# The edge stage of a graph attention layer rewritten: direct gather indices, four slots, messages in place, half-rows with their weights, and the carried row as one more edge

## Chip, core and metric

The kernel runs on one core of a Trainium2 chip. The metric is the device time of one execution in microseconds (us), the median of several runs. The engines named below are TensorE (PE), VectorE (DVE), ScalarE (ACT), GpSimd (POOL) and SyncE (SP); SP and POOL issue the DMAs of this kernel.

## The reference

6250 nodes with 512 features, 100000 edges sorted by their destination `dst`, with random sources `src`. Everything is f32. After the graph layer stands a small per-node network, which the change touches only where it reads the sums.

```python
h = leaky_relu(layernorm(x) @ W.T + b, 0.2).reshape(N, 8, 64)
e_src = sum(h * w_att_src, -1);  e_dst = sum(h * w_att_dst, -1)
e = leaky_relu(e_src[src] + e_dst[dst], 0.2)
m = segment_max(e, dst);  ex = exp(e - m[dst]);  s = segment_sum(ex, dst)
a = ex / s[dst] * dist
x = x + segment_sum(h[src] * a[:, :, None], dst).reshape(N, 512)
# then x = x + ffn(layernorm(x)): decode, three small layers, one-hot codes added
```

## The kernel before, in words

Three stages follow one another, with a short preparation between the first two.

**Nodes** (`project`, 49 tiles of 128 nodes): layer norm, the 512x512 product, leaky relu, and the two scores of each head. A row of 520 f32 (512 values and 8 source scores, 2080 bytes) goes to the table `h` in HBM. `prepare` then computes, for each group of edges, the first destination (`bases`), every edge's destination relative to it (`rel`), and a table of shifts for each node (`shifts`).

**Edges** (`attend_windows`): 112 groups of 7 tiles of 128 edges. All destinations of a group lie in one window of 128 nodes that begins at the group's base. For a group g the engines do this:

- ACT copies 7 columns of source indices into `src_idx` (`set_src`). POOL waits for that copy, then issues 7 indirect DMAs (L768), each of which fetches 128 rows of `h` into a slot of `gathered`. There are three slots. From the fourth group on POOL also waits until the messages of the group that had the slot are made.
- DVE compares node numbers with `rel` and gives the 0/1 matrix `member16` (L778, bf16, 128x896). ACT widens it to f32 (`member`), PE transposes it (L873), ACT copies the transpose (`turn_member`, `memberT`), and PE multiplies it with the window of shifts (`at_edges`, L864), which looks up the destination's numbers for every edge.
- DVE sums the three bf16 parts of that result (`at_dst`, L786), adds the source scores, makes the leaky relu and the difference; ACT takes the exponential `ex` and splits off its bf16 parts together with DVE (L819, L824); DVE makes the coefficients and seven messages into a buffer of its own (`w_msg`, L810).
- PE adds up (`add_up`): per tile an f32 product of `member` and the 512 message columns (L886, recorded as two passes a tile), and then seven small bf16 products for the sums of the weights (L893).
- ACT takes the sum out of PSUM into `summed` (`evacuate`), DVE reduces the three parts of the weights into it (L831), and then adds the first row of the next window as it stood in HBM (`carried`, L841): two groups' windows overlap in one node, and SP loads that one row (L752) after the store of the group before has landed (L751). SP then stores 128 rows into `agg` (L741). So there is a chain from group to group: `carried` -> store -> landing -> load of one row -> landing -> `carried`.

Each engine has a fixed order for one round u: ACT `set_src(u+1)`, `exps(u-1)`, widen(u), exponent part (u-1), `turn_member(u)`, `evacuate(u-3)`; PE `at_edges(u-1)`, first half of `add_up(u-2)`, transposes(u), second half of `add_up(u-2)`; DVE `carried(u-4)`, scores(u-1), member(u), messages(u-1), weights(u-3); SP window load(u), row load(u-4), store(u-4). The first nine groups and the last four are written out; between them a loop of three groups a turn runs.

**Finish** (13 chunks of up to 4 tiles): divides by the sum of the weights, adds to x, and runs the small network, with f32 products on PE (L1197, L1208).

Of the kernel before, what the change touches and what calls it, by code (L numbers as in the profile page):

```python
# [22 lines left out]
P = 128  # L23
# [9 lines left out]
ROW = D + HEADS  # L33
GROUP = 7
GROUPS = -(-E // (P * GROUP))
# [20 lines left out]
CHUNKS = NODE_TILES // CHUNK  # L56

# [49 lines left out]
def project(nc, top, banks, t, keep):  # L107

    with ExitStack() as ctx:
# [49 lines left out]
        with nc.Block() as block:  # L159
# [40 lines left out]
            def _(pool):  # L200
# [3 lines left out]
                for n, s in turns(pool, NODE_TILES):  # L204
# [3 lines left out]
                    nc.gpsimd.tensor_tensor(prod_dst[:, s, :], hrow[:, s, 0:D], w_dst[:, :],  # L208
# [3 lines left out]
            def _(dve):  # L212
# [17 lines left out]
                def scores(n, s):  # L230
# [6 lines left out]
                    nc.vector.tensor_tensor(hrow[:, s, 0:D], leak[:, s, :], ps_h[s][:, :], ALU.max).then_inc(s_row, 1)  # L237
# [3 lines left out]
                    nc.vector.tensor_tensor(prod_src[:, :], hrow[:, s, 0:D], w_src[:, :], ALU.mult  # L241
                                            ).then_inc(s_psrc, 1)
                    dve.wait_ge(s_psrc, n + 1)
                    nc.vector.tensor_reduce(hrow[:, s, D:ROW], prod_src[:, :].rearrange("p (h d) -> p h d", h=HEADS),
                                            AX, ALU.add).then_inc(s_esrc, 1)
# [54 lines left out]
            def _(act):  # L300
# [12 lines left out]
                def keep_src(n, s):  # L313
                    act.wait_ge(s_esrc, n + 1)
                    nc.scalar.activation(keep["esrc"][:, bass.ds(n * HEADS, HEADS)], hrow[:, s, D:ROW], ACT.Copy
                                         ).then_inc(s_kept, 1)
# [18 lines left out]
def attend_any(nc, top, banks, t, keep, branch_semaphores):  # L335
# [3 lines left out]
    with ExitStack() as ctx:  # L339
# [50 lines left out]
        with nc.Block() as block:  # L390
# [31 lines left out]
            def _(dve):  # L422
                dve.wait_ge(s_load, 16)

                def heads(ap):
                    return ap.rearrange("p (h d) -> p h d", h=HEADS)

                for n in edge_turns(dve):
# [5 lines left out]
                    if reused(n, 1):  # L434
# [22 lines left out]
                    step("score", nc.vector.tensor_tensor(score[:, :], grow[:, D:ROW], mrow[:, HEADS:2 * HEADS],  # L457
                                                          ALU.add))
# [7 lines left out]
                    for b in range(2):  # L466
# [4 lines left out]
                        if b == 0:  # L471
# [17 lines left out]
                    nc.vector.tensor_tensor(heads(msg[:, :]), heads(grow[:, 0:D]),  # L489
                                            coef[:, :].unsqueeze(2).to_broadcast([P, HEADS, HD]), ALU.mult  # L490
                                            ).then_inc(done["msg"], 1)
                    dve.wait_ge(s_a, 16 * (n + 1))
                    nc.vector.tensor_tensor(heads(arow[:, 0:D]), heads(arow[:, 0:D]),
                                            exps[:, 0:HEADS].unsqueeze(2).to_broadcast([P, HEADS, HD]),
                                            ALU.mult).then_inc(s_scaled, 1)
# [149 lines left out]


def attend_windows(nc, top, banks, t, keep, branch_semaphores):

    with ExitStack() as ctx:
        def sb(name, shape, dt=F32):
# [850 lines left out]
```

## Time and profile before

| | us |
|---|---|
| median of 3 runs | 2029.5 |
| lowest and highest | 2019.91 and 2036.35 |
| the profiled execution: its own time | 2030.48 |
| its span, first to last instruction | 2028.7 |
| node stage and preparation, in the span | 0 to 354 |
| edge stage | 354 to 1718 |
| finish | 1718 to 2028.7 |

The durations that follow come from the one profiled execution. Its own time is 1.8 us above its span and 1.0 us above the median. The edge stage takes 1364 of the 2028.7 us, 12.18 us for each of 112 groups. The mean granted clock of TensorE over the span was 0.852 of full speed.

### The profile page before, as it was taken

Reading aid. Unit: us, or ns where it says so; the run is one execution under the profiler, and the core shown is the slowest. Engines: PE = TensorE matmul, PEld = TensorE weight load, DVE = VectorE, ACT = ScalarE, POOL = GpSimd, SP = SyncE. Lnnn points to the kernel's source line nnn. Section 1 sums busy time; section 2 is a strip of 40 time slices with the busy share of each in tenths; the row PEclk is TensorE's granted clock in tenths of the full one; section 3 lists DMA queues with packets and bytes.
Section 4 is the critical chain, followed back from the end, with each engine's and each line's share of the span. In section 5 each row is a group of like instructions: output and inputs, shape, how many; then the busy total and the mean of one; then the engine's idle time right before and its main releaser. Section 6 shows DMA issues by size and latency. Waiting matters only on the chain. (4 is left out here: it accounts for less than half of the span.)

```text
span 2028.7 us, 24635 instructions
## 1 busy us (share of the span) xinstructions
PE 1406.5 (69%) x5502; PEld 662.8 (33%) x5502; DVE 1337.0 (66%) x3092; ACT 496.3 (24%) x1141; POOL 986.9 (49%) x932
## 2 busy tenths in 40 slices
PE   5778783477666676566767676766657665299997
PEld 2333331233232233232323232323223332155555
DVE  5777776467566576665766576666657655868784
ACT  1222220222222222222322222222222221123332
POOL 1222221666656566575556755666666651213231
PEclk9999987688888898888888888888889878578888
DMA  5333333666665566575566765666666653424331
GB/s 216 131 124 126 125 125 64 166 195 191 176 175 172 169 191 191 168 200 168 160 172 194 199 171 159 191 178 174 172 188 182 188 165 91 176 89 167 145 135 67
DMA packets 151399, 326.44 MB, mean 161 GB/s; under 512 B 47312, under 2 KB 47568, under 8 KB 151246
## 3 DMA queue, kind: packets, MB, share of 16 engines
q0 software_dynamic: 62720, 208.78, 37.1%
q1 hardware_dynamic: 88654, 117.38, 17.2%
q8 instruction: 9, 0.15, 0.0%
q14 instruction: 16, 0.13, 0.0%
HBM read 255.82 MB, written 70.27 MB: 161 GB/s over the span
## 5 line engine op out<-in xcount | busy, mean ns | idle before, releaser
L768 POOL DMA_INDIRECT gathered<-table_h,w_src_idx x784 | 827.5, 1055 | 517.2 <-issue 244.3
L886 PE MATMUL bank<-w_msg,member 128*128 128x512 f32 x1568 | 810.3, 662 | 0.0
L810 DVE TENSOR_TENSOR w_msg<-gathered,w_coef 128x512 f32<-128x512 f32 x784 | 489.8, 694 | 3.9
L886 PEld LDWEIGHTS bank<-w_msg,member 128*128 128x128 f32 x1568 | 313.8, 213 | 316.3 <-issue 282.2
L873 PE MATMUL bank<-ident,member 128*128 128x128 bf16 x784 | 72.0, 240 | 313.8 <-DVE member L778 221.2
L786 DVE TENSOR_REDUCE at_dst<-bank 128x112 f32<-128x336 f32 x112 | 56.3, 503 | 326.8 <-remote 259.5
L277 PE MATMUL bank<-wt,xnT 128*128 128x512 f32 x392 | 203.0, 666 | 0.0
L208 POOL TENSOR_TENSOR prod_dst<-hrow,w_dst 128x512 f32<-128x512 f32 x49 | 75.6, 1543 | 250.4 <-DVE hrow L237 250.4
L920 ACT ACTIVATE w_ex<-w_diff 128x56 f32<-128x56 f32 x112 | 27.9, 249 | 673.2 <-issue 348.0
L873 PEld LDWEIGHTS bank<-ident,member 128*128 128x128 bf16 x784 | 53.5, 108 | 402.6 <-DVE member L778 221.4
L1197 PE MATMUL bank<-h,w 128*128 128x512 f32 (+1 forms) x338 | 180.3, 682 | 0.0
L841 DVE TENSOR_TENSOR summed<-summed,w_carry 1x520 f32<-1x520 f32 x111 | 76.4, 688 | 155.7 <-ACT summed L908 126.4
L1114 POOL TENSOR_TENSOR res<-x_in,y 128x2048 f32<-128x2048 f32 (+1 forms) x13 | 61.9, 4765 | 234.9 <-DMA out<-res 162.8
L908 ACT ACTIVATE memberT<-bank 128x896 bf16<-128x896 bf16 x112 | 102.1, 911 | 266.0 <-remote 239.3
L778 DVE TENSOR_TENSOR member<-node_no,k_rel 128x896 bf16<-128x896 f32 x112 | 122.1, 1090 | 9.6 <-DMA node_no<-in_node_no 9.6
L908 ACT ACTIVATE member<-member 128x896 f32<-128x896 bf16 x112 | 106.5, 951 | 64.0 <-issue 35.0
L864 PE MATMUL bank<-window,memberT 128*128 128x48 bf16 x784 | 40.3, 190 | 117.4 <-ACT memberT L908 94.8
L277 PEld LDWEIGHTS bank<-wt,xnT 128*128 128x128 f32 x392 | 78.0, 209 | 95.7 <-issue 95.7
L1197 PEld LDWEIGHTS bank<-h,w 128*128 128x128 f32 x338 | 68.8, 223 | 64.3 <-issue 62.3
L286 PE MATMUL bank<-ident,xn 128*128 128x128 f32 x196 | 32.3, 289 | 78.7 <-DVE xn L227 78.7
L1143 ACT ACTIVATE h<-bank,b 128x512 f32<-128x512 f32 (+1 forms) x65 | 41.7, 661 | 162.7 <-PE bank L1208 90.6
L1208 PEld LDWEIGHTS bank<-w,h 128*128 128x128 f32 x490 | 72.0, 225 | 21.7 <-issue 20.9
(133 smaller groups left out, 1185.8 us busy)
## 6 DMA issues: line engine op xcount, KB each, us to landing
table_agg<-summed SPq DMA_DIRECT2D x112, 260.0 KB
table_agg<-zeros SPq DMA_DIRECT2D x50, 260.0 KB, 2.2
table_h<-hrow SPq DMA_DIRECT2D x49, 260.0 KB, 2.1
xt<-in_x SPq DMA_DIRECT2D x49, 256.0 KB, 2.7
gathered<-table_h,w_src_idx POOLq DMA_INDIRECT x784
agg_in<-table_agg SPq DMA_DIRECT2D x12, 1040.0 KB, 7.7
x_in<-in_x SPq DMA_DIRECT2D x12, 1024.0 KB, 5.4
out<-res SPq DMA_DIRECT2D x12, 1024.0 KB, 4.4
```

The lines of the kernel that those rows point to most:

```text
L208: nc.gpsimd.tensor_tensor(prod_dst[:, s, :], hrow[:, s, 0:D], w_dst[:, :], ALU.mult).then_inc(s_pdst, 1)
L277: mm = nc.tensor.matmul(ps_h[s][:, :], xnT[:, s, c * P:(c + 1) * P], wt[:, c, :], start=False, stop=(c == DC - 1))
L768: pool.indirect_dma_start(out=gathered[:, s, j, :], out_offset=None, in_=t["h"][:, :], in_offset=bass.IndirectOffsetOnAxis(ap=src_idx[:, s ...
L778: nc.vector.tensor_tensor(member16[:, s, :, :], node_no[:, :].unsqueeze(1).to_broadcast([P, GROUP, P]), keep["rel"][:, bass.ds(g * GROUP, ...
L810: nc.vector.tensor_tensor(msg[:, s, j, :].rearrange("p (h d) -> p h d", h=HEADS), gathered[:, s, j, 0:D].rearrange("p (h d) -> p h d", h=H ...
L841: nc.vector.tensor_tensor(summed[0:1, s, :], summed[0:1, s, :], carry[:, :], ALU.add).then_inc(d["carried"], 1)
L873: last = nc.tensor.transpose(member_t[:, j * P:(j + 1) * P], member16[:, s, j, :], ident16[:, :])
L886: nc.tensor.matmul(sums[s][:, :], member[:, s, j, :], msg[:, s, j, :], start=first, stop=final)
L908: return nc.scalar.activation(out, in_, ACT.Copy)
L1114: nc.gpsimd.tensor_tensor(res[:, s, 0:k, :], x[:, s, 0:k, :], y[:, s, 0:k, :], ALU.add).then_inc(d["res"], 1)
L1197: last = nc.tensor.matmul(bank[:, 0:w], w2[:, weights, :], h1[:, units, 0:w], start=(i == 0), stop=(i == len(pairs) - 1))
L1208: last = nc.tensor.matmul(y3[:, 8 * j:8 * j + 8], h2[:, g, j * P:(j + 1) * P], w3[:, g, :], start=(g == 0), stop=(g == 4))
```

## The change

- The two halves of a row carry their own weights: a row is 2 x (256 values + 4 scores), still 520 f32. `project` and `finish` read and write it through split views.
- POOL gathers straight from the index table; the copy `src_idx` and the wait for it are gone. It waits for the sums of the group that had the slot. There are four slots.
- The exponentials go into the four score columns of each half of the gathered row, and the messages overwrite the gathered values in place. PE then adds up values and weights in one product for each half: two f32 products of 260 columns a tile in place of one of 512 and one small bf16 one. The bf16 parts of `ex`, L819, L824, L831 and L893 are gone.
- The carried row becomes an edge: slot 32 of tile 0 in each group stays free of edges (895 edges a group, still 112 groups), its `rel` is set to 0, and SP loads the row of `agg` into `gathered[32, slot, 0]` after the message of tile 0 is made. PE adds tile 0 last, when that row has landed. L841 is gone.
- The lookup (member, transposes, `at_edges`) runs one group ahead of the scores, with two PSUM banks for its result. The operands `coef` and `node_no` move to PSUM.
- All rounds are written out, without a loop. The window load runs two groups ahead.

The diff, cut to its core:

```diff
             def _(pool):
-                for g, s in rounds(pool, 0):
-                    wait_alone(pool, s_idx, g + 1, s_pool_on)
+                for g in range(GROUPS):
+                    s = g % S
                     if old(g):
-                        wait_alone(pool, d["msg"], GROUP * (g - 2), s_pool_on)
+                        wait_alone(pool, d["sums"], g - S + 1, s_pool_on)
                     for j in range(GROUP):
                         pool.indirect_dma_start(
                             out=gathered[:, s, j, :], out_offset=None, in_=t["h"][:, :],
-                            in_offset=bass.IndirectOffsetOnAxis(ap=src_idx[:, s, j:j + 1], axis=0)
-                        ).then_inc(s_g[s], 48)
+                            in_offset=bass.IndirectOffsetOnAxis(ap=keep["src"][:, g, j:j + 1], axis=0)
+                        ).then_inc(s_g[s], 16)
...
+                def carry_in(g, s):
+                    to = gathered[CARRY_ROW:CARRY_ROW + 1, s, 0, :]
...
+                    base = base_of(g)
+                    before = (s - 1) % S
+                    sp.wait_ge(s_put[before], filled(g - 1, 16))
+                    sp.wait_ge(d["msg"], g * GROUP + 1)
+                    sp.dma_start(to, t["agg"][bass.ds(base, 1), :]).then_inc(s_carry, 16)
+
+                for u, slot in rounds(2, 1):
+                    stage(u, slot, -2, load_window)
+                    stage(u, slot, 1, store)
+                    stage(u, slot, 0, carry_in)
...
                     for j in range(GROUP):
+                        values = row_values(gathered[:, s, j, :])
                         nc.vector.tensor_tensor(
-                            msg[:, s, j, :].rearrange("p (h d) -> p h d", h=HEADS),
-                            gathered[:, s, j, 0:D].rearrange("p (h d) -> p h d", h=HEADS),
-                            coef[:, j, :].unsqueeze(2).to_broadcast([P, HEADS, HD]), ALU.mult
-                        ).then_inc(d["msg"], 1)
+                            values, values, by_half(coef[:, j * HEADS:(j + 1) * HEADS]).unsqueeze(3)
+                            .to_broadcast([P, 2, HEADS // 2, HD]), ALU.mult).then_inc(d["msg"], 1)
...
+                for u, slot in rounds(1, 0):
+                    stage(u, slot, 0, scores)
+                    stage(u, slot, -1, make_member)
+                    stage(u, slot, 0, messages)
...
+                def add_tile(g, s, j, start, stop):
+                    for a in range(2):
+                        last = nc.tensor.matmul(sums_of(s)[:, a, :], member[:, s, j, :],
+                                                gathered[:, s, j, a * HALF:(a + 1) * HALF], start=start, stop=stop)
+                    return last
+
+                def add_first(g, s):
+                    pe.wait_ge(d["member"], g + 1)
+                    if old(g, 2):
+                        pe.wait_ge(d["evac"], g - 1)
+                    for j in range(1, 5):
                         pe.wait_ge(d["msg"], g * GROUP + j + 1)
+                        add_tile(g, s, j, j == 1, False)
+
+                def add_rest(g, s):
+                    for j in range(5, GROUP):
+                        pe.wait_ge(d["msg"], g * GROUP + j + 1)
+                        add_tile(g, s, j, False, False)
+                    pe.wait_ge(s_carry, 16 * (g + 1))
+                    add_tile(g, s, 0, False, True).then_inc(d["sums"], 1)
 
                 pe.wait_ge(s_i16, 1)
+                for u, slot in rounds(1, 0):
+                    stage(u, slot, -1, transpose)
+                    stage(u, slot, 0, add_first)
+                    stage(u, slot, -1, at_edges)
+                    stage(u, slot, 0, add_rest)
...
+                for u, slot in rounds(1, 1):
+                    stage(u, slot, 0, exps)
+                    stage(u, slot, 1, evacuate)
+                    stage(u, slot, -1, widen_member)
+                    stage(u, slot, -1, turn_member)
```

## Rows read from the trace of the kernel before

**Rows 1.** The page, part 1: busy time, share of the span and instructions of each engine.

```profile
PE 1406.5 (69%) x5502; PEld 662.8 (33%) x5502; DVE 1337.0 (66%) x3092; ACT 496.3 (24%) x1141; POOL 986.9 (49%) x932
```

**Rows 2.** Busy time in the edge stage: PE, PEld, DVE, ACT, POOL, clock, DMA share, GB/s.

```profile
354.00:1718.00 1364.00, 902.70 (x3920) 412.37 (x3920) 862.32 (x1903) 343.62 (x786) 827.45 (x784) 0.85 0.62 176
```

**Rows 3.** Groups of instructions: busy us, mean ns of one | idle before, its enders.

```profile
L768 POOL DMA_INDIRECT gathered<-table_h,w_src_idx x784 | 827.5, 1055 | 517.2 <-issue 244.3 <-DVE w_msg L810 149.0 <-ACT w_src_idx L908 123.9
L886 PE MATMUL bank<-w_msg,member 128*128 128x512 f32 x1568 | 810.3, 662 | 0.0
L810 DVE TENSOR_TENSOR w_msg<-gathered,w_coef 128x512 f32<-128x512 f32 x784 | 489.8, 694 | 3.9
L886 PEld LDWEIGHTS bank<-w_msg,member 128*128 128x128 f32 x1568 | 313.8, 213 | 316.3 <-issue 282.2 <-DVE w_msg L810 34.0
...
L841 DVE TENSOR_TENSOR summed<-summed,w_carry 1x520 f32<-1x520 f32 x111 | 76.4, 688 | 155.7 <-ACT summed L908 126.4 <-issue 11.6 <-DVE summed L831 10.0
...
L908 ACT ACTIVATE summed<-bank 128x512 f32<-128x512 f32 x112 | 66.2, 591 | 10.0 <-PE bank L893 10.0
...
L893 PE MATMUL bank<-w_ex,member 128*128 128x24 bf16 x784 | 37.3, 174 | 56.1 <-issue 30.3 <-DVE summed L831 25.8
...
L819 DVE TENSOR_TENSOR w_ex_rest<-w_ex 128x56 f32<-128x56 f32 x112 | 23.3, 208 | 0.6 <-ACT w_ex L908 0.6
```

**Rows 4.** Waits in the edge stage: us in total, times, longest us.

```profile
DVE at_dst L786 <- remote: 259.5, 42, 13.1
...
ACT memberT L908 <- remote: 239.3, 48, 12.1
```

**Rows 5.** The timeline of PE: start us, us, instruction, count, [idle before].

```profile
514.10 0.19 PEld L886 LDWEIGHTS bank<-w_msg,member 128*128 128x128 f32 x1 [0.24 <-issue]
...
516.58 0.34 PE L864 MATMUL bank<-window,memberT 128*128 128x48 bf16 x7
...
550.37 0.56 PE L873 MATMUL bank<-ident,member 128*128 128x128 bf16 x7 [1.08 <-issue]
```

**Rows 6.** The timeline of POOL in the same stretch.

```profile
527.09 0.95 POOL L768 DMA_INDIRECT gathered<-table_h,w_src_idx  x1 [0.30 <-issue]
537.27 1.10 POOL L768 DMA_INDIRECT gathered<-table_h,w_src_idx  x1 [9.23 <-DVE w_msg L810]
```

**Rows 7.** The timeline of DVE and of ACT: what waited for those PE instructions.

```profile
529.59 0.51 DVE L786 TENSOR_REDUCE at_dst<-bank 128x112 f32<-128x336 f32 x1 [12.37 <-remote]
...
532.14 4.30 DVE L810 TENSOR_TENSOR w_msg<-gathered,w_coef 128x512 f32<-128x512 f32 x7
...
558.91 0.92 ACT L908 ACTIVATE memberT<-bank 128x896 bf16<-128x896 bf16 x1 [7.39 <-remote]
```

**Rows 8.** The timeline at the stage's start: first and seventh gather, first scores.

```profile
356.80 1.70 POOL L768 DMA_INDIRECT gathered<-table_h,w_src_idx  x1 [16.93 <-issue]
...
365.07 0.95 POOL L768 DMA_INDIRECT gathered<-table_h,w_src_idx  x1 [0.30 <-issue]
...
368.95 0.51 DVE L786 TENSOR_REDUCE at_dst<-bank 128x112 f32<-128x336 f32 x1 [11.61 <-DMA gathered<-table_h,w_src_idx]
```

**Rows 9.** The timeline: store and row load of SP twice, then the last L841.

```profile
892.61 0.42 SPq L741 DMA_DIRECT2D table_agg<-summed  x1
...
897.32 0.06 SPq L752 DMA_DIRECT2D w_carry<-table_agg  x1
...
1713.48 0.42 SPq L741 DMA_DIRECT2D table_agg<-summed  x1
1715.76 0.28 SPq L752 DMA_DIRECT2D w_carry<-table_agg  x1
...
1717.21 0.69 DVE L841 TENSOR_TENSOR summed<-summed,w_carry 1x520 f32<-1x520 f32 x1 [2.87 <-DMA w_carry<-table_agg]
```

**Rows 10.** The timeline of PE in the finish: twenty f32 passes of 8 columns.

```profile
1909.40 2.40 PE L1208 MATMUL bank<-w,h 128*128 128x8 f32 x20
```

More of the change, by code:

```diff
@@ L32 @@
 DC = D // P
[L33 removed]
+HALF = D // 2 + HEADS // 2
+ROW = 2 * HALF
 GROUP = 7
[L35 removed]
+CARRY_ROW = 32
+GROUP_EDGES = P * GROUP - 1
+GROUPS = -(-E // GROUP_EDGES)
 EDGE_TILES = GROUPS * GROUP
@@ L691, in attend_windows @@
-        s_g = [sem(f"w_gathered{i}") for i in range(S3)]
-        s_put = [sem(f"w_stored{i}") for i in range(S3)]
-        s_carry = sem("w_carry_copied")
-        s_win = [sem(f"w_window_loaded{i}") for i in range(S3)]
-        names = ("member16 member member_t memberT edge_dst at_dst score leaky diff ex ex_hi ex_rest ex_mid ex_lo "
-                 "coef msg sums evac evac_w carried").split()
-        d = {k: sem("w_" + k) for k in names}
-        def filled(g, slot, per):
-            return (g - slot) * (per // S3) + per
@@ new lines, in attend_windows, with filled, sums_of, edge_dst @@
+        names = ("member16 member member_t memberT edge_dst at_dst score leaky diff ex coef msg sums evac").split()
+        d = {k: sem("w_" + k) for k in names}
+        def filled(g, per):
+            return per * (g // S + 1)
+        def sums_of(slot):
+            return psum[:, 2 * (slot % 2):2 * (slot % 2) + 2, 0:HALF]
+        def edge_dst(slot):
+            return psum[:, 6 + slot % 2, 0:GROUP * PARTS]
+        def rounds(lead, drain):
+            for u in range(-lead, GROUPS + drain):
+                yield u, u % S
@@ L713, in stage, with old @@
         def stage(u, slot, lag, do):
-            if isinstance(u, int) and not 0 <= u - lag < GROUPS:
+            if not 0 <= u - lag < GROUPS:
                 return
-            do(u - lag, (slot - lag) % S3)
-        def old(g):
-            return reused(g, S3)
+            do(u - lag, (slot - lag) % S)
+        def old(g, slots=S):
+            return g >= slots
         with nc.Block() as block:
@@ L754, in _ @@
-                for u, slot in rounds(sp, 4):
-                    stage(u, slot, 0, load_window)
-                    stage(u, slot, 4, load_carry)
-                    stage(u, slot, 4, store)
-                for g in range(GROUPS - S3, GROUPS):
-                    sp.wait_ge(s_put[g % S3], filled(g, g % S3, 48))
+                    base = base_of(g)
+                    if old(g, 1):
+                        before = (s - 1) % S
+                        sp.wait_ge(s_put[before], filled(g - 1, 16))
@@ L868, in transpose @@
                 def transpose(g, s):
                     pe.wait_ge(d["member16"], g + 1)
-                    if not (isinstance(g, int) and g == 0):
+                    if old(g, 1):
                         pe.wait_ge(d["memberT"], g)
@@ L898, in _, with at_edges @@
-                pe.wait_ge(s_i16, 1)
-                for u, slot in rounds(pe, 2):
-                    stage(u, slot, 1, at_edges)
-                    stage(u, slot, 2, lambda g, s: add_up(g, s, 0))
-                    stage(u, slot, 0, transpose)
-                    stage(u, slot, 2, lambda g, s: add_up(g, s, 1))
+                def at_edges(g, s):
+                    pe.wait_ge(d["memberT"], g + 1)
+                    pe.wait_ge(s_win[s], filled(g, 16))
+                    if old(g, 2):
+                        pe.wait_ge(d["at_dst"], g - 1)
+                    for j in range(GROUP):
+                        last = nc.tensor.matmul(edge_dst(s)[:, j * PARTS:(j + 1) * PARTS], memberT[:, s, j, :],
+                                                window[:, s, :], start=True, stop=True)
+                    last.then_inc(d["edge_dst"], 1)
```

291 lines of the change are left out of this document (110 added, 181 removed).

## The prediction

> **What bounds the kernel now.** I read the page first: no engine is full, PE 69% and DVE 66% of the span [rows 1]. Such means hide the stages, so I asked for the busy times of each stage. In the edge stage PE works 902.7, DVE 862.3 and POOL 827.5 of 1364 us, the DMA engines 0.62 of the time [rows 2]. Nothing is busy for two thirds of 12.18 us a group, so the pace comes from waits, and the list of waits [rows 4] is what the reader has to look at.
>
> POOL's own time is this. An indirect DMA takes 1.055 us on average and is followed by 0.29 us of idle time put down to issue: 244.3 us [rows 3] less the 16.9 us before the very first [rows 8], over 784. So seven take 7 x 1.345 = 9.4 us. When nothing else runs they come 1.25 us apart (0.95 and 0.30, the rows of 365.07 and 527.09 [rows 6, 8]), which is 8.75 us a group. The other 272.9 us are waits: 149.0 for the messages of the group that had the slot and 123.9 for ACT's copy of the indices [rows 3], 2.4 us a group. 9.4 + 2.4 = 11.9, and the rest of the 12.18 is the fill and the drain.
>
> Behind both waits stands a third thing. DVE's `at_dst` waits 259.5 us and ACT's `memberT` 239.3 us for something that the profile calls remote, which here means a semaphore change that it can't put beside the end of an instruction [rows 4]. Both wait for PE. The seven products L864 are recorded from 516.58 to 516.92, and `at_dst`, which needs them, starts at 529.59; the transposes of 550.37 to 550.93 are followed by `memberT` at 558.91 [rows 5, 7]. In the first case POOL issued gathers without a pause until 528.04, stopped because the messages (they begin 2.6 us after the scores and take 4.3 us [rows 7]) were not made, and went on at 537.27 [rows 6]. So PE's results are reported late while gathers run, up to 13 us, and the report comes soon after the run of gathers has ended. I can't tell the mechanism from this trace. It costs 498.8 us of waits in 90 pieces, 4.45 us a group, of which before only a part lies on the path.
>
> At the Trainium skill, SBUF — State Buffer, "Who interferes with whom", PE never waits on anyone and DMA never contends with a compute engine. By that rule nothing of these 498.8 us comes from the gathers, and a change of slots would leave them. The rows show late PE results in the edge stage and can't say of which port or queue they come, so I take the rule neither for nor against.
>
> **The change, part by part, in the edge stage.** I count the pace T of a group and then 112 T.
>
> POOL. The copy of the indices and its wait (123.9 us) go, and nothing takes their place: the table is in SBUF before the stage. The wait for the messages becomes a wait for the sums of g-4. After the late report of the example the old kernel needed 7.7 us until POOL went on (529.59 to 537.27, scores and messages of that group) [rows 6, 7]. In the new one the sums of the group four back are already added up when the stall begins, and only their report is late, so POOL goes on right after it. What stays of such a gap is the time from the last gather's end to the report, 1.5 us in the example, and some of what ACT and DVE then do. I allow 1 to 4 us and take 2.5. With 2.5 us for each of some 45 stalls (half the 90 pieces, as both engines wait in a stall) that is 112 us or 1.0 us a group, in place of 2.4.
>
> How long the gathers themselves take: between 8.75 us bare and 9.4 us as now. The excess of 0.11 us on the mean DMA is spent where DVE works, and DVE loses L841 (76.4 us) [rows 3]; I take the middle, 9.1 us. At the Trainium skill, SBUF — State Buffer, "Who interferes with whom", a `tensor_tensor` with one input in PSUM leaves GpSimd's port free, and descriptor generation is held up by two-port copies, not by `tensor_tensor`. By it `node_no` in PSUM changes nothing for the gathers and 9.4 would stay, 34 us more in all.
>
> DVE loses L841 (0.69 us), L819 (0.21) and L824 and L831, which are of L819's size or less: about 1.3 us a group [rows 3]. It keeps 862.3 - 141 = 721 us, 6.4 us a group [rows 2], with seven messages of 0.69 us as the largest part. In place or from PSUM they cost what they cost now, give or take 0.05 us each, since nothing of their shape changes; at worst 0.35 us a group, beneath POOL.
>
> PE loses L893 (37.3 us). A tile's two passes of 512 columns become four of 260. At full clock a 512-column pass is 0.43 us (0.19 of a load and 0.24 until the next [rows 5]; the load, 213 ns on average [rows 3], lies beside it), so 260 columns are 0.22 us and 28 of them 6.1 us, against 6.0 now. That holds if the weight load, which is now done 28 times, hides behind 260 columns. Twenty f32 passes of 8 columns take 2.40 us, 0.12 each [rows 10], and there is nothing in them but loads: a load needs 0.12 us of the array, about half of 0.22. I take it as hidden, with 28 x 0.12 = 3.4 us a group as the other end. With the transposes and lookups, 0.56 + 0.34 us [rows 5], PE has 7.0 us a group, or 10.4 at that other end.
>
> ACT loses `src_idx` and two small copies, and isn't near the path.
>
> The new chain from group to group, which now runs through PE, is the new cost. After the sums of g-1: ACT takes them out, 0.59 us [rows 3], and SP issues the store some 0.2 us later (an estimate, half the 0.42 us of an issue [rows 9]). From store to row load it is 2.3 us at the end of the stage, where no gather runs (1713.48 to 1715.76), and 4.7 in the midst of them (892.61 to 897.32) [rows 9], though this second one has a window load between the two. From the row load to its use it is 1.45 us at the end [rows 9]; in the midst of gathers I have no clean row, and bound it by 1.45 and 2.4 us (longer by as much as the store, 2.4, would be 3.85 at the very most). Then PE adds tile 0, 4 x 0.22 = 0.9 us. The sum is 5.4 us quiet and 0.59 + 0.2 + 4.7 + 2.0 + 0.9 = 8.4 us loaded. Under 9.1 it is hidden behind the gathers, but with little to spare, and PE's late reports now stand inside it: the wait of ACT's `evacuate` for the sums, which holds `widen` and `turn` of the next group behind it on ACT, and PE's own wait for the row, behind which the next group's transposes stand. That ordering is what the lookup one group ahead has to pay for: it gives DVE scores that don't wait for PE in the same round, and hides stalls of up to about one group's messages (4.3 us).
>
> The row layout in `project` and `finish` changes no size: messages split over 8 heads and plain 512-column operations take the same 0.69 us now. I cost it at nothing, with +-5 us for the split views. Code without a loop: the first nine groups were written out already and no slower, +-5 us. The waits of SP on its queue: behind the store's wait stand the window load two groups ahead and the row load, and neither is late by that.
>
> **The sum.** Outside the edge stage 2028.7 - 1364 = 664.7, and 1.8 between span and time. The stage begins 3 us before the first gather. After the last gather come 3.9 us to the scores (365.07 to 368.95 [rows 8]), 2.6 us to the first message and 4.3 us of messages [rows 7], and one chain of 5.4 us: 16 us. Time = 666.5 + 19 + 112 T. With T = 9.1 + 1.0 = 10.1: 685.5 + 1131 = 1817 us, and I say 1820. The profiled execution stands 1.0 us above the median, which is nothing here.
>
> **Rivals.**
> 1. PE's weight loads don't hide. T = 10.4 by PE alone, and with 1.0 us of what a stall leaves 11.4; halfway, 10.9: 1906 us. For it: 28 loads of 0.19 to 0.21 us in passes of 0.22. Against it: the 0.12 us of the array. At the Trainium skill, TensorE: Matmul & The Clock Gate, "Part 3: Packing small matmuls", loads overlap with running matmuls only when their row groups differ, and that is this rival; the trace's loads, recorded inside passes spaced 0.43 us [rows 5], speak against it.
> 2. Slower: the chain through PE takes the place of the waits removed. Each late report is paid in full, once a group, since sums, store, row and sums follow on each other: 8.4 + 4.45 = 12.85, 2125 us. It decides from T = 12.0, that is from 3.6 us of late reports a group in the chain. For it: longer runs of gathers, since four slots let POOL run ahead up to 28 gathers, and late reports come in long runs. Against it: not each late report is that of the sums, and a stall fills slots that are then worked off at 8.4 or less.
> 3. The change doesn't do what it says: the late reports set the pace as before (PE reports only when the gathers stop, so groups in a run come at the pace of stalls), T = 11.9 to 12.2, 2018 to 2052 us, within 1%.
> 4. Late reports vanish with the waits: T = 8.75 to 9.1, 1665 to 1705 us. It is the low end of the forecast.
>
> **Numbers.** About 1% is what a measurement of this kernel can tell from no change. Forecast with its low end (T from 8.9 to 10.7, 1680 to 1885): 0.66. Rival 1 (T up to 11.4, 1885 to 1960): 0.14. Rival 3: 0.06, within 1%. Rival 2: 0.14, slower. Faster by over 1% 0.80, within 1% 0.06, slower 0.14. The range of 8 in 10 is that of the forecast and rival 1, 1680 to 1960.
>
> **What would show it.** POOL's gathers should come to 1.25 to 1.35 us apart, with idle time beyond that of 1 us a group put down to the sums; DVE's busy time in the stage near 720 us; L841, L819, L824, L831 gone; f32 passes near 0.22 us apart at full clock, and the granted clock above 0.85 of the stage. If passes come 0.34 us apart, rival 1 is right. If SP's stores follow each other at the same 12 us as before, with PE waiting for the row load, rival 2 is. The prediction fails if late reports are caused by something that the new order makes worse, as I only know when they happen and not why.

## The result, and the profile after

The changed kernel took 1942.51 us (median of 4, 1933.15 to 1954.28), the kernel before 2024.7 us beside it. The ratio is 0.9626, with a 95% interval of 0.953 to 0.9722: faster, by some 80 us and not by the 210 forecast. The profiled execution took 1940.52 us. The page, part 1, of the changed kernel:

```profile
PE 1412.5 (73%) x6286; PEld 968.7 (50%) x6286; DVE 1211.7 (62%) x2647; ACT 439.4 (23%) x805; POOL 901.2 (46%) x932
```

The edge stage now lies from 352 to 1638 us (columns as in [rows 2]):

```profile
352.00:1638.00 1286.00, 915.06 (x4704) 721.52 (x4704) 736.67 (x1457) 286.42 (x450) 741.68 (x784) 0.87 0.66 188
```

POOL's 827.5 us of [rows 2] are 741.7, DVE's 862.3 are 736.7: both saved what they were meant to. The stage got only 78 us shorter. The groups of instructions, to be read beside [rows 3]:

```profile
L879 PE MATMUL bank<-gathered,member 128*128 128x260 f32 x3136 | 845.1, 426 | 110.0 <-DVE gathered L843 75.7 <-issue 30.1 <-ACT member L908 2.4
L800 POOL DMA_INDIRECT gathered<-table_h,k_src x784 | 741.7, 946 | 525.4 <-issue 237.6 <-PE bank L879 144.7 <-remote 143.1
```

A gather takes 946 ns where it took 1055, the bare value. The two waits of POOL that the change removed (149.0 and 123.9 us) are gone, and 144.7 + 143.1 = 287.8 us stand in their place, both for the sums of PE: the first where the profile finds the report beside the end of PE's last product, the second where it doesn't. The list of waits, beside [rows 4] (us in total, times, longest):

```profile
DVE at_dst L818 <- remote: 328.6, 53, 21.9
...
POOL gathered L800 <- PE bank L879: 144.7, 42, 5.6
POOL gathered L800 <- remote: 143.1, 55, 5.5
```

POOL waits 42 + 55 = 97 times in 112 groups, so now nearly every group has its stall. The timeline shows one cycle (start us, us, instruction, [idle before]):

```profile
1049.16 0.95 POOL L800 DMA_INDIRECT gathered<-table_h,k_src  x1 [2.35 <-remote]
...
1051.73 3.16 PE L879 MATMUL bank<-gathered,member 128*128 128x260 f32 x12
...
1056.66 0.95 POOL L800 DMA_INDIRECT gathered<-table_h,k_src  x1 [0.30 <-issue]
1059.22 0.60 ACT L908 ACTIVATE summed<-bank 128x520 f32<-128x520 f32 x1 [5.69 <-remote]
...
1060.00 0.94 POOL L800 DMA_INDIRECT gathered<-table_h,k_src  x1 [2.39 <-remote]
```

PE's last pass of the sums ends at 1054.89. ACT, which by its order waits for these sums next, goes on at 1059.22, 1.6 us after POOL's seven gathers have ended (1057.61), and POOL goes on 0.8 us later. One cycle is 8.45 + 2.39 = 10.84 us. Now and then a stall is long, as in this stretch:

```profile
1008.43 3.74 PE L879 MATMUL bank<-gathered,member 128*128 128x260 f32 x16 [0.63 <-ACT summed L908]
...
1012.02 0.34 PE L872 MATMUL bank<-window,memberT 128*128 128x48 bf16 x7
...
1020.59 0.94 POOL L800 DMA_INDIRECT gathered<-table_h,k_src  x1 [0.30 <-issue]
1024.12 0.51 DVE L818 TENSOR_REDUCE at_dst<-bank 128x112 f32<-128x336 f32 x1 [12.84 <-remote]
...
1025.02 0.94 POOL L800 DMA_INDIRECT gathered<-table_h,k_src  x1 [3.49 <-remote]
```

The lookup is done at 1012.36; `at_dst` starts 11.8 us later, 2.6 us after a run of gathers has ended that is longer than one group's.

### The profile page after: what moved, and what is told of

Same layout as the page of the kernel before. It is cut to its first block and busy times, and to the rows that moved or that the text cites. A ratio compares the mean times of both kernels' runs of the same rounds, so it can differ in the third digit from the quotient of the medians.

```text
span 1938.9 us, 22591 instructions
## 1 busy us (share of the span) xinstructions
PE 1412.5 (73%) x6286; PEld 968.7 (50%) x6286; DVE 1211.7 (62%) x2647; ACT 439.4 (23%) x805; POOL 901.2 (46%) x932
## 5 line engine op out<-in xcount | busy, mean ns | idle before, releaser
L800 POOL DMA_INDIRECT gathered<-table_h,k_src x784 | 741.7, 946 | 525.4 <-issue 237.6
L879 PE MATMUL bank<-gathered,member 128*128 128x260 f32 x3136 | 845.1, 426 | 110.0 <-DVE gathered L843 75.7
L879 PEld LDWEIGHTS bank<-gathered,member 128*128 128x128 f32 x3136 | 643.1, 212 | 241.3 <-issue 73.3
L843 DVE TENSOR_TENSOR gathered<-gathered,bank 128x512 f32<-128x512 f32 x784 | 478.7, 683 | 3.8
L912 ACT ACTIVATE gathered<-w_diff 128x56 f32<-128x56 f32 x112 | 27.9, 249 | 786.0 <-DVE w_diff L831 397.4
L317 PE MATMUL bank<-wt,xnT 128*128 128x512 f32 x392 | 199.0, 655 | 0.0
L811 DVE TENSOR_TENSOR member<-bank,k_rel 128x896 bf16<-128x896 f32 x112 | 121.3, 1083 | 0.0
L908 ACT ACTIVATE summed<-bank 128x520 f32<-128x520 f32 x112 | 67.1, 599 | 154.2 <-remote 112.4
L326 PEld LDWEIGHTS bank<-ident,xn 128*128 128x128 f32 x196 | 21.9, 143 | 115.6 <-DVE xn L266 69.1
```

Of the source, the lines that this page charges most:

```text
L317: mm = nc.tensor.matmul(ps_h[s][:, :], xnT[:, s, c * P:(c + 1) * P], wt[:, c, :], start=False, stop=(c == DC - 1))
L800: pool.indirect_dma_start(out=gathered[:, s, j, :], out_offset=None, in_=t["h"][:, :], in_offset=bass.IndirectOffsetOnAxis(ap=keep["src"][ ...
L811: nc.vector.tensor_tensor(member16[:, s, :, :], node_no.unsqueeze(1).to_broadcast([P, GROUP, P]), keep["rel"][:, g * GROUP:(g + 1) * GROUP ...
L843: nc.vector.tensor_tensor(values, values, by_half(coef[:, j * HEADS:(j + 1) * HEADS]).unsqueeze(3) .to_broadcast([P, 2, HEADS // 2, HD]), ...
L879: last = nc.tensor.matmul(sums_of(s)[:, a, :], member[:, s, j, :], gathered[:, s, j, a * HALF:(a + 1) * HALF], start=start, stop=stop)
L908: return nc.scalar.activation(out, in_, ACT.Copy)
```

## The experiments

The theory after the first result, the **lock**: while POOL issues gathers, PE's completion reports are held back, and come some 1.5 us after the run of gathers ends. Since POOL now starts a group on such a report, POOL and PE wait for each other once a group. Rivals: the chain through the carried row sets the pace; the traffic of the gathers, and not their issuing, holds the reports back. No run took POOL's wait for the sums away, which would have tried the lock itself.

The runs came in seven sets, each on one chip with the kernel before beside them. I hadn't expected what the sets did: in two of them the kernel before took 2000 and 1999 us, in five 1806 to 1812, and every kernel of a set followed. Chips 6 and 10 each gave one set of either kind, so it is not the chip alone. I call them **late sets** (as the first measurement) and **prompt sets**, by what the traces show: in each trace of a late set there are waits put down to "remote", in none of a prompt set.

| kernel | late sets: us, ratio to before (95%) | prompt sets: us, ratio to before (95%) |
|---|---|---|
| changed | 1918.5, 0.9617 (0.9531 to 0.9703) | 1650.5, 0.9128 (0.9083 to 0.9173) |
| no carried row | 1913.6, 0.9632 (0.9526 to 0.9737) | 1655.4, 0.9191 (0.9135 to 0.9247) |
| 80 B rows | 1938.0, 0.9729 (0.9637 to 0.9821) | 1667.2, 0.924; 1662.2, 0.9205 |
| operands in SBUF | 1917.4, 0.9615; 1912.5, 0.9641 | 1729.7, 0.9534 (0.9488 to 0.958) |
| direct indices only | 2037.6, 1.0209 (1.0101 to 1.0316) | 1807.8, 1.0014 (0.9985 to 1.0043) |
| rows issued by SP | none | 1691.9, 0.9382; 1692.0, 0.9368; 1688.1, 0.9359; 1687.6, 0.9311 |
| plain copies on POOL | none | 1797.2, 0.992 (0.9878 to 0.9962) |
| pause in each run | none | 2097.3, 1.1551 (1.1492 to 1.161) |

**Small rows.** Traffic against issuing.

```
-    out=gathered[:, s, j, :], out_offset=None, in_=t["h"][:, :],
+    out=gathered[:, s, j, 250:270], out_offset=None,
+    in_=t["h"].rearrange("r (x c) -> (r x) c", c=20),
```

DVE also sets `gathered` to zero once before the first gather, which makes POOL wait 32 us at the start of the stage; the cut above leaves that out.

> The changed kernel with one edit: each of the 784 gathers fetches 20 elements (80 B) per row in place of 520 (2080 B), by the same indices, so the traffic of the gathers falls to a twenty-sixth while GpSimd issues as many of them as before; the rest of each row stays zero, so the output is not the attention's. Two theories of why PE's completion reports come late during a run of gathers. If the traffic holds them back, they become prompt here, GpSimd's waits for the sums (2.57 us per group in the changed kernel) go, and the edge stage runs at 8.45 to 8.75 us per group: 685 + 112 x 8.45..8.75, some 1630 to 1670 us. If GpSimd's own work of making the gathers holds them back, nothing changes: reports made from 4 us into a run on still come 1.5 us after it, one group takes 10.85 to 11.4 us, some 1900 to 1945 us.

The set was a prompt one: 1667.2 us, reports prompt. Taken alone it would have looked as if the traffic were the cause; the kernel before at 1806 us in the same set forbade that reading. The second try met a prompt set again (1662.2 us):

> The same edit as in the earlier run with gathers of 80 B per row, for the case that this set has late reports. If the gathers' traffic holds PE's reports back: prompt reports, 8.75 us per group, some 1665 us, even where the kernel before takes 2000 us. If GpSimd's making of the gathers does: reports from 4 us into a run on still late, 1900 to 1945 us. In a set with prompt reports: 1665 us again, which tells nothing new.

The third met a late set:

> Gathers of 80 B per row once more, for a set with late reports (kernel before at 1970 us or more). If the gathers' traffic holds the reports back: 1660 to 1670 us, a ratio near 0.83, and no report late. If GpSimd's making of the gathers does: near the changed kernel's 1920 us, ratio 0.95 to 0.97, reports late from 4 us into a run on. In a set with prompt reports: 1665 us again.

1938.0 us. The stage, its busy times and its waits:

```profile
352.00:1635.00 1283.00, 908.24 (x4704) 715.37 (x4704) 749.13 (x1458) 286.05 (x449) 742.48 (x784) 0.88 0.16 32
```
```profile
DVE at_dst L820 <- remote: 296.3, 35, 22.9
...
POOL gathered L801 <- remote: 142.8, 54, 5.3
```

The DMA engines are busy for 0.16 of the stage in place of 0.66, 32 GB/s in place of 188, and the late reports are all there. The traffic doesn't hold them back; that rival falls. The 20 us over the changed kernel's 1918.5 (in the other late set) are less than the 33 us that POOL waits here for the zeros.

**No carried row.** The chain from group to group is cut.

```
-    sp.wait_ge(s_put[before], filled(g - 1, 16))
     sp.wait_ge(d["msg"], g * GROUP + 1)
-    sp.dma_start(to, t["agg"][bass.ds(base, 1), :]).then_inc(s_carry, 16)
+    sp.dma_start(to, t["h"][NODES:NODES + 1, :]).then_inc(s_carry, 16)
```

> The changed kernel with one edit: the row that is carried into the group as an extra edge is always the table's row of zeros and is loaded without waiting for the store of the group before (so sums of a node that lies in two groups lose a part). This cuts the chain from group to group through the store, the row's load, PE's last pass and the sums. The theory that this chain sets the pace (the rival of the prediction, 12.85 us per group when PE's reports are late): 9 to 10.5 us per group, 1690 to 1860 us. The theory that GpSimd and PE wait for each other, because GpSimd starts a group only on the report of the sums and PE's report comes only after GpSimd's run of gathers: the last pass is done earlier, but its report still comes after the run: unchanged, 1920 to 1960 us, with the gaps of 2.4 us on GpSimd still there.

> The same edit as in the earlier run without the carried row (always the row of zeros, no wait for the store), now beside the changed kernel itself on one chip. If GpSimd's gathers bound the stage there, the same time as the changed kernel within 1%. If the chain through the carried row bounds it, 3 to 10% less. On a chip with late reports: within 1.5% of the changed kernel if the report after the run is what starts the next run, much less if the chain is.

In a late set 1913.6 against 1918.5 us of the changed kernel in the same set, in a prompt one 1655.4 against 1650.5 of another set. Taking the chain away gains nothing in either; my prediction's second rival falls. POOL's stalls stay without it, 155.0 + 109.4 = 264 us against 128.7 + 143.3 = 272 of the changed kernel in the same set:

```profile
POOL gathered L797 <- PE bank L876: 155.0, 43, 6.2
...
POOL gathered L797 <- remote: 109.4, 44, 5.2
```

**The changed kernel in both conditions.**

> The changed kernel itself, beside the kernel before on the same chip, because the runs so far were made on a chip where the kernel before takes 1806 us and not 2025, and where no report of PE came late in the two runs with indexed gathers. If the late reports are a matter of the chip, then on a chip with prompt reports GpSimd runs gather after gather at 8.75 us per group: 685 + 112 x 8.75, some 1650 to 1680 us, 0.92 of the kernel before. If they are a matter of the kernel (what small rows or the missing carry had taken away), GpSimd still waits 2.4 us per group here and the ratio is again 0.953 to 0.972. On a chip where the kernel before takes over 2000 us: 0.953 to 0.972, as measured.

> The changed kernel once more. The kernel without the carried row took 1655 us in one set of runs (kernel before 1806 us, no report of PE late) and 1914 us in another (kernel before 2000 us, reports late), so the chip as it was given to a set has two conditions, and the changed kernel has been timed in the late one alone. If this set has prompt reports: 1650 to 1680 us, ratio 0.91 to 0.93, GpSimd's gathers in one run of some 981 us. If it has late ones: ratio 0.953 to 0.972 as twice before.

The first of these met a late set: 1918.5 us, 0.9617. The second met a prompt one, 1650.5 us and 0.9128. Its stage, POOL's gathers, and the same place of the timeline as the long stall above:

```profile
352.00:1350.00 998.00, 837.18 (x4704) 664.51 (x4704) 736.46 (x1457) 281.46 (x448) 742.16 (x784) 0.97 0.83 241
```
```profile
L800 POOL DMA_INDIRECT gathered<-table_h,k_src x784 | 742.2, 947 | 255.3 <-issue 243.7
```
```profile
1008.29 3.75 PE L879 MATMUL bank<-gathered,member 128*128 128x260 f32 x16 [0.82 <-DVE gathered L843]
...
1011.87 0.34 PE L872 MATMUL bank<-window,memberT 128*128 128x48 bf16 x7
...
1012.24 0.51 DVE L818 TENSOR_REDUCE at_dst<-bank 128x112 f32<-128x336 f32 x1 [1.11 <-PE bank L872]
```

PE's sixteen passes take 3.75 us here and 3.74 there, and the lookup ends at 1012.21; here `at_dst` starts 0.03 us after it, there 11.8 us. The same program, the same instructions, another delivery of the report. POOL issues all 784 gathers in one run from 353.1 to 1333.8 us, 8.76 us a group.

**Operands in SBUF.** Does the place in PSUM shorten the gathers, and is that worth anything?

```
-    coef = psum[:, 5, 0:GROUP * HEADS]
-    node_no = psum[:, 5, GROUP * HEADS:GROUP * HEADS + P]
+    coef = sb("w_coef", [P, GROUP * HEADS])[:, :]
+    node_no = sb("node_kept", [P, P])[:, :]
```

> The changed kernel with one edit: node_no and the coefficients lie in SBUF as in the kernel before, not in PSUM, so DVE's member, coefficient and message operations read two SBUF operands. If it was their place in PSUM that took the mean gather from 1055 to 946 ns, it goes back: 112 x 7 x 0.109 = 85 us where GpSimd is the bound (4.4 to 5.2% slower than the changed kernel), the gathers that lie over a message operation being the long ones. If the collisions were with GpSimd's or DVE's other work that the change removed: the same time as the changed kernel within 1%, gathers at 946 ns.

> The changed kernel with node_no and the coefficients in SBUF, once more. With late reports it took as long as the changed kernel (1917 and 1919 us) though its mean gather was 1009 ns against 947. If this set has prompt reports (kernel before near 1807 us), the gathers set the pace, and their length must show: 784 x 0.062 us = 49 us over the changed kernel's 1650, some 1700 us, ratio 0.935 to 0.945; if the longer gathers cost nothing there either, 1650. With late reports: 0.96 again.

> The changed kernel with node_no and the coefficients in SBUF, for a set with prompt reports. There the gathers run without a gap, 8.76 us per group in the changed kernel (947 ns each, 1650 us) and 10.06 in the kernel before with direct indices (1133 ns each, 1808 us). If the operands in PSUM are what shortened them, the collisions come back for node_no and the coefficients: 1060 to 1133 ns each, 9.5 to 10.06 us per group, 1735 to 1800 us. If something else in the change did it (copied messages, summed in two parts): below 1010 ns and 1700 us. In a set with late reports: 0.96 again.

In both late sets the time is that of the changed kernel, though the mean gather went from 947 to 1009 ns (1013 in the second): 49 us more of POOL's work come out of its stalls, which fall from 272 to 214 us. In a prompt set the kernel takes 1729.7 us, between the two expectations and nearer to the first, and 79 more than the changed one:

```profile
L800 POOL DMA_INDIRECT gathered<-table_h,k_src x784 | 811.8, 1035 | 256.1 <-issue 253.0
```

The gathers cost 811.8 - 742.2 = 70 us more, and that is nearly all of the 79. They are long where DVE reads two operands from SBUF (POOL's timeline, then DVE's):

```profile
1010.45 0.95 POOL L800 DMA_INDIRECT gathered<-table_h,k_src  x1 [0.30 <-issue]
1011.70 1.37 POOL L800 DMA_INDIRECT gathered<-table_h,k_src  x1 [0.30 <-issue]
```
```profile
1011.16 1.08 DVE L811 TENSOR_TENSOR member<-node_kept,k_rel 128x896 bf16<-128x896 f32 x1
1012.16 0.21 DVE L836 TENSOR_TENSOR w_coef<-gathered,k_dist 128x56 f32<-128x56 f32 x1
1012.41 0.69 DVE L843 TENSOR_TENSOR gathered<-gathered,w_coef 128x512 f32<-128x512 f32 x1
```

By the starts and ends of all records, some 100 gathers lie over these three lines together and take 1.42 us on average; in the changed kernel's prompt set such gathers take 0.95. The same records say when a gather gets long. Of 784, 206 take over 1 us; in 205 of these a member or message operation had begun before the gather and still ran 0.2 us after its start, and of the 578 others that is so for one. A long gather ends 0.82 us after that operation's end (0.81 to 0.82 in nearly all). In the changed kernel's prompt set 355 gathers lie so, and one is long. Of the 70 us, 49 come from `member` (`node_no`) and 21 from the messages (the coefficients).

**Direct indices only.** One part of the change on the kernel before.

```
-    for g, s in rounds(pool, 0):
-        wait_alone(pool, s_idx, g + 1, s_pool_on)
+    for g in range(GROUPS):
+        s = g % S3
...
-    ap=src_idx[:, s, j:j + 1]
+    ap=keep["src"][:, g, j:j + 1]
```

> The kernel before with one part of the change alone: GpSimd's gathers take their indices from the kept table and its loop is written out, so it waits for no index copy; three slots, copied messages and everything else stay. Where the pace is set by late reports of PE (a chip where the kernel before takes over 2000 us): the same within 1% of the kernel before, since the wait for the index copy is not what starts GpSimd again. Where reports are prompt and gathers bound the stage: faster only by what waits and reads of indices cost between gathers, 0 to 0.4 us per group, 0.975 to 1.0 of the kernel before; the rest of the gain comes from the shorter gathers.

> The kernel before with direct indices alone, once more, for the case that this set has prompt reports (kernel before near 1807 us): 112 x (0 to 0.4) us less than the kernel before, 0.975 to 1.0, which would leave the other 0.06 to 0.08 of the gain to the rest of the change. With late reports: 1.01 to 1.03 as before.

In a late set this is 2% slower than the kernel before (1 to 3% by the interval), which I hadn't expected: the wait for the index copy is gone, and the wait for the messages, 149.0 us in [rows 3], is now 292.2. In a prompt set it is the kernel before to 0.14%. Its gathers there:

```profile
L768 POOL DMA_INDIRECT gathered<-table_h,k_src x784 | 888.6, 1133 | 255.6 <-issue 255.6
```

That is 888.6 + 255.6 us, one run, 10.06 us a group. So POOL sets the pace of this kernel and of the changed one in prompt sets (the kernel before itself has no trace there), and nearly the whole difference is the length of the gathers: 888.6 - 742.2 = 146 of the 157 us. Here 328 gathers take over 1 us. By the same reading of the records, 62 us of the excess go with `member`, 36 with the messages and 48 with L841, which adds two operands from SBUF and which the change took out.

**Without indexed gathers.** Plain copies of 128 rows, from POOL and from SP.

```
-    pool.indirect_dma_start(out=gathered[:, s, j, :], ..., in_=t["h"][:, :], in_offset=...)
+    at = (g * GROUP + j) % NODE_TILES * P
+    pool.dma_start(gathered[:, s, j, :], t["h"][at:at + P, :])     # or sp.dma_start
```

> The changed kernel with one edit: GpSimd issues the same number of transfers of the same 128 rows of 2080 B into the same places, but as plain copies of 128 rows that follow each other in the table, without an index (so other rows than the edges' are summed). Same bytes, far less work on GpSimd per transfer. If the traffic holds PE's reports back, they stay late, and the stage stays near 11 us per group (1900 to 1960 us). If GpSimd's making of indexed gathers (946 ns each) holds them back, they are prompt; what sets the pace then is the next in line, DVE's 6.4 us or PE's 7 us per group, or the landing of the rows: 7.5 to 9.5 us per group, 1525 to 1750 us.

> As the run with plain copies, but the copies are issued by SP and GpSimd does nothing in the edge stage (rows that follow each other are loaded in place of the edges' rows). If GpSimd's issuing is what holds PE's reports back, in whatever form, no report of PE is late here, and a group takes 7.5 to 9.5 us (1525 to 1750 us); if the traffic does it, reports stay late as in the changed kernel and the time is 1900 to 1960 us.

> Plain copies of as many rows issued by SP, GpSimd idle in the edge stage, once more. With prompt reports it took 1692 us. In a set with late ones (kernel before at 1970 us or more): if GpSimd's own issuing is what holds PE's reports back, 1680 to 1710 us again, a ratio near 0.85, no report late; if whatever is late there is late without GpSimd too, 1900 us or more.

> Plain copies issued by SP, GpSimd idle, for a set with late reports (kernel before at 1970 us or more). If GpSimd's own issuing holds PE's reports back: 1680 to 1710 us, a ratio near 0.85, no report late. If they are late without GpSimd: 1900 us or more. In a set with prompt reports: 1692 us again.

> Plain copies issued by SP, GpSimd idle, once more for a set with late reports (kernel before at 1970 us or more). If GpSimd's own issuing holds PE's reports back: 1680 to 1710 us, a ratio near 0.85, no report late. If they are late without GpSimd: 1900 us or more. In a set with prompt reports: 1690 us again.

All five met prompt sets, so they say nothing of late reports. From POOL a group takes (1797 - 685)/112 = 9.9 us, more than I allowed:

```profile
1002.71 3.70 POOL L801 DMA_DIRECT2D gathered<-table_h  x7 [5.91 <-PE bank L877]
1013.54 3.71 POOL L801 DMA_DIRECT2D gathered<-table_h  x7 [7.12 <-PE bank L877]
```

POOL needs 3.7 us for seven copies, and then waits for the sums, while PE waits 255.2 us for the carried row. From SP it is 9.0 us a group, with 167 us of PE's waits for that row. That the chain through the carried row bounds these two is read from the waits and not shown; no run took it away there.

**A pause in each run.**

```
+    if j == 4:
+        wait_alone(pool, s_g[s], filled(g, 16 * GROUP) - 16 * 3, s_pool_on)
```

> The changed kernel with one wait more: GpSimd waits after the fourth gather of each group until these four have landed, so no run of gathers is longer than 4 (4.8 us). If reports are held back only from some 4 us into a run on, few are late in a set with late reports, and a group takes 8.45 us of gathers, 2 to 3 us of the new wait and what is left of the old one: 10.5 to 12 us per group, 1860 to 2030 us, with hardly a report over 2 us late. If they are held back for as long as the sums of these four groups are open, whatever the runs: late reports as before, and the wait's 2 to 3 us on top, 13 us per group, 2140 us. In a set with prompt reports there are only the new waits: 10.5 to 11.5 us per group, 1860 to 1970 us.

A prompt set again, and above what I expected for one: the fourth gather lands later than I had thought.

```profile
999.53 0.95 POOL L802 DMA_INDIRECT gathered<-table_h,k_src  x1 [0.30 <-issue]
1004.87 0.94 POOL L802 DMA_INDIRECT gathered<-table_h,k_src  x1 [4.39 <-DMA gathered<-table_h,k_src]
```

4.3 us for a pause on average (482.1 us in 112), 12.6 us a group, where I had allowed 2 to 3 us and 11.5. Whether shorter runs keep reports prompt in a late set wasn't seen.

## Why the prediction was wrong

The direction was right, and that gathers get shorter with less of DVE's work beside them; the size was not. That 1942.51 lies in 1680 to 1960 is luck: the forecast proper ended at 1885, and the part from there to 1960 was given to weight loads that don't hide, which the trace shows hidden. Term by term, from the profiled execution:

| term, us | forecast | measured |
|---|---|---|
| outside the stage | 666.5 | 1940.5 - 1286 = 654.5 |
| fill and drain | 19 | 1286 - 962 - 288 = 36 |
| gathers with their issue | 112 x 9.1 = 1019 | 741.7 + 237.6 - 16.9 = 962 |
| POOL's stalls | 45 x 2.5 = 112 | 97 x 2.97 = 288 |

Stalls cost 176 us more than forecast and fill and drain 17 more, the gathers 57 less and the rest 12 less: 123 us above 1817.

**The step that failed** is "What stays of such a gap", with its premise that "the sums of the group four back are already added up when the stall begins, and only their report is late". I took half of 90 waits as stalls, 45 of 2.5 us; there are 97 of 2.97 us on average. By the starts and ends of the records (98 stalls over 0.5 us by this count) the premise holds in 51, and there a stall takes 2.4 us in the median, near what I had allowed. In the other 47 PE was not done with those sums when POOL stopped. These take 3.6 us in the median and 160 of the 288 us, and in 36 of them the scores of that same group had begun over 2 us after their lookup was recorded as done, in the 51 only in 4. So a late report costs twice: at the sums, and one step earlier at the lookup, where it pushes back scores, messages and sums.

Why there are so many is argued from the cycle above: a new run of seven gathers begins as soon as one report arrives, and the next group's lookup and sums aren't reported until it is over. The fourth slot doesn't help. In 109 of 112 groups the two groups before have not begun their scores when POOL begins, so all four slots are taken in each stall. That POOL went on right after the report, which I counted as the gain, is what closes the lock. Then POOL's account is not a sum of costs: in late sets 49 us of longer gathers are paid out of the stalls, as the two runs with operands in SBUF show, so the gathers' saving can't simply be credited with the 80 us. Direct indices alone aren't the source either (2% slower). That it is the shorter restart is only argued, from the rows: 7.7 us from a late `at_dst` to POOL's next gather before [rows 6, 7], 0.9 us after (1024.12 to 1025.02).

**The gathers.** "The middle, 9.1" was half the right thing. They fell to the bare 8.75, because the DVE operations that had made them long were given an operand in PSUM (`member`, messages) or taken out (L841). At the Trainium skill, SBUF — State Buffer, "Who interferes with whom", a `tensor_tensor` with both inputs in SBUF contends with what GpSimd reads, and one with a single SBUF input does not. The runs agree with both halves: 1035 ns with the operands in SBUF, 947 in PSUM. The product for the coefficients, whose inputs lie in SBUF in either kernel, takes 0.21 us and made none of the 100 gathers over it long in the changed kernel's prompt set (0.95 us). What I made of it in the prediction, that descriptor generation is outside that rule and `node_no` in PSUM changes nothing, is refuted: these two operands are worth 79 us in a prompt set.

**PE.** Passes come 3.74/16 = 0.234 us apart with loads of 0.21 beside them; the first rival (loads that don't hide, 1906 us) gave nearly the right time for a wrong reason. DVE's busy 736.7 us are 2% over the 721 forecast. The chain's 5.4 to 8.4 us weren't measured; without the chain the time is the same. "With little to spare" holds: in a prompt set PE waits 72.6 us for the carried row.

**Rivals.** The second (each late report paid once a group in the chain through PE) had the lock's rhythm but the wrong chain: taking the carried row away changes nothing. The third came nearest to what happens in a late set, where late reports do set the pace, but at 11.2 us a group and not 11.9 to 12.2 (1942.5 less 685.5, over 112). The fourth (late reports vanish, 1665 to 1705 us) is what prompt sets show, at 1650: I held it for an end of one forecast, and it is a condition that came with the session, whichever kernel ran. The trace of before could show only one of the two conditions, and my range of 1680 to 1960 spans nearly what the changed kernel does in both.

**Open.** What sets the condition; the same chip had both. Which part of the change brings the 80 us of a late set. Which part of GpSimd's work delays PE's reports: the traffic is excluded, and the kernel that issues from SP, which would have told it, met four prompt sets. Nor is it shown by an experiment that the issuing is the cause at all; for it stands only that the reports come when runs of gathers end. The lock itself is read from the records too: no run let POOL go on without the sums' report.

## What to carry to other kernels

Before a wait on PE is put in front of a queue of gathers, look in the trace at when PE's reports come: a longer queue of work didn't help here, where the report that refills it came mostly when the queue was empty. Ask of each wait in the forecast whether only the report is late or the work too. Where GpSimd's gathers set the pace, count the long DVE operations with two SBUF operands that run when a gather begins, and put one operand in PSUM. And time a change beside the old kernel in more than one session before its size is believed: here it is 3.8% or 8.7%.

## What the runs showed of the hardware

The same kernel runs in 1650 or 1918 us by the session, with DVE's, ACT's and POOL's busy time in the stage within 2% of each other; the ratio of a kernel to the one before is steady to 1% among sets of one kind. What differs in the traces is the delivery of PE's semaphore reports while GpSimd issues. By the semaphore records of the changed kernel's first trace, matched in order to the ends of PE's products: of the reports that PE makes in the first 4 us of a run of gathers 1 of 82 is over 2 us late, of those from 4 to 8 us into a run 85 of 111, of those made later in longer runs 16 of 29, and outside runs 2 of 237 (130 of these in the finish, where nothing is gathered). Of the 104 late ones 50 come 1.4 to 1.8 us after a run's end. Only PE's are late: no recorded update of ACT or DVE in the stage comes over 0.1 us after its instruction's end, in four late traces and three prompt ones. But the late traces lack many of them (of DVE's 1456 in the changed kernel's first trace 878 are there), where its prompt trace has all but one. What that means is open.

In the changed kernel the granted clock in the stage is 0.87 in the late trace and 0.97 in the prompt one (means between the levels of 2.4 and 1.2 GHz). In prompt sets it is 0.94 with the operands in SBUF and 0.80 in the kernel with pauses. It is lower where the stage takes longer for the same products (998 us at 0.97, 1073 at 0.94, 1286 at 0.87, 1438 at 0.80), and goes with the waits, not with the set.
